# A fused attention and lookup block on one core: v projected in two portions around the first loads, its bias carried through the output projection

## The chip, the core and the metric

The kernel runs on one core of a Trainium2 chip. The metric is device time of one execution in microseconds (us); lower is better. Three runs of the kernel before gave 3075.67, 3077.20 and 3077.66 us, median 3077.2 us.

## The reference, cut to what matters

The input x is 4096 tokens of 256 channels. All arrays are float32.

```
xn  = layernorm(x)
q, k, v = split(xn @ w_qkv + b_qkv)          # 16 heads of 16 channels each
attn = softmax(q @ k.T / 4) @ v               # per head, 4096 x 4096 scores
y   = attn @ w_proj + b_proj
x   = x + layernorm(y)
h   = layernorm(x)                            # then a lookup in 1024 keys with the 8 best kept,
x   = x + layernorm(h + gate(h) * (softmax(top8(scores(h))) @ values))
```

The weights of a softmax row add up to 1, so a bias b_v added to every row of v comes out of the attention as b_v added to every row of attn. Hence (attn + b_v) @ w_proj + b_proj is attn @ w_proj + (b_v @ w_proj + b_proj).

## The kernel before, in words

The program of each engine is written out by hand, and the engines are tied by semaphores. Every engine works its program strictly in the order written. The token axis is cut into 32 tiles of 128 rows, and into 8 chunks of 4 tiles.

**First stage.** SP issues eight loads of x (L296), POOL issues the loads of w_qkv (L358), of the q and k bias (L359), and two broadcast loads of the v bias into `bv` (L361), then builds the identity and, from L388, the first 1/sqrt(variance) (`powers`, L380 and L382). DVE normalises a chunk (L748), TensorE transposes it (L1086), ACT keeps the transpose in `xnT` (L512), and TensorE projects q and k for it in four matrix products of two matmuls (`project_qk`, L1094). ACT evacuates each product twice (L520, L522), DVE takes the difference (L754), so that each of q and k is held as a rounded part and a rest, and SP stores both to DRAM (L302).

**Loads of the first head.** Scores and maxima are computed from stacks of such parts (`q_stack`, `k_stack`), read back from DRAM by `load_first` on SP: 12 transfers (L307), six of them for the maxima (semaphore `first_max_in`), then six for the scores (`first_score_in`).

**v.** Meanwhile ACT copies the normalised transposes into `v_src`, two buffers of one chunk (`copy_xnT`, L538), TensorE projects v (`project_v`, L1108: a loop over 8 chunks, with two pairs of tiles in each, four matmuls to a pair) into PSUM banks 4 and 5, and ACT evacuates each pair into `v_all` (`evacuate_v`, L544). POOL clears rows of the stacks (L398, L401), adds the bias to each pair of v tiles (L412), and copies the first head's v into `v_head` (`copy_v`, L405). All of v is projected before the first maximum.

**First maximum pass.** The softmax needs the maximum of each score row ahead of time. A piece is two matmuls of 512 columns (`max_half`, L1135) into one of two pairs of PSUM banks, and one reduction of 1024 columns on DVE (`row_max`, L797); 16 pieces and one small reduction (L804) make the 512 maxima of a query chunk. Before the main loop two whole chunks are done (AHEAD = 2), and half of the third (LEAD = 8 pieces): 40 pieces. POOL splits the negated maxima into three bf16 parts (`split_max`, L421 to L431) and TensorE puts them into rows (`max_row`, L1186), the first of them in bank 5, for which it waits on `v_evac`.

**Main loop.** 64 iterations (16 heads by 4 pairs of query chunks) of 32 steps. A step has two scores (L1161), two exponentials on ACT (L568), four products with v (L1170), and one further piece of a maximum (L1135, L797).

**Last iteration and second stage.** In the last iteration no maxima are left, and other work stands between the steps: `transpose_weights` (L1266 to L1269), `route_weights` (L1275, L1277), the transposes of attn, and `project_out` (L1294). DVE copies the weights out of PSUM (L948 to L954) and adds `bproj` to the projections (`projected`, L818). Then come the norms and the lookup to the end. The weights of this stage are loaded by SP behind `w3_init` (L327), which POOL raises as it fills small tensors (L449 to L454), more than 100 us ahead of their use.

Of the kernel before, what the change touches and what calls it, by code (L numbers as in the profile page):

```python
# [23 lines left out]
P = 128  # L24
# [10 lines left out]
def sandwich_kernel(nc, x, w_qkv, b_qkv, w_proj, b_proj, q_proj_w, router_w, aux_keys, aux_values,  # L35
# [46 lines left out]
        return S_BANK[(RING * it + at) % SRING]  # L82

    W3_LOADS = 14
    LOAD_EVERY = 4
    RUS = 64
    MASKROW = RD
# [6 lines left out]
    with ExitStack() as ctx:  # L94
# [3 lines left out]
        def sem(name):  # L98
            return ctx.enter_context(nc.semaphore(name))
# [29 lines left out]
        nm_parts = sb("nm_parts", [P, TPC, MROWS], BF16)  # L129
        rinv = sb("rinv", [P, 2, 4])  # L130
        lead = sb("lead", [P, 1])

        v_rows = v_all[:, :].rearrange("p (t c) -> p t c", c=C)

# [1 line left out]
        xn = work[:, 0:1024].rearrange("p (t c) -> p t c", t=TPC)  # L136
        wqkv = work[:, 2048:3584].rearrange("p (k n) -> p k n", k=CC)
        qk_f32 = k_raw[:, 0:4 * CH].rearrange("p (g t) -> p g t", g=4)
        bv = work[:, 3584:4096].rearrange("p (a c) -> p a c", a=2)
        bqk = work[:, 4096:4100]  # L140
        xnT = attn[:, 0:NC * CC * CH].rearrange("p (c k t) -> p c k t", c=NC, k=CC)
        v_src = [work[:, 1024 * b:1024 * (b + 1)].rearrange("p (k t) -> p k t", k=CC) for b in range(2)]
# [4 lines left out]
        hT = work[:, 5120:6144].rearrange("p (k t) -> p k t", k=CC)  # L147
        ru = work[:, 6144:6656]
        g1T = k_raw[:, 2048:2560]
        o2 = [work[:, 1024 * b:1024 * (b + 1)].rearrange("p (t c) -> p t c", t=TPC) for b in range(4)]  # L150
        res = [v.rearrange("p (t c) -> p t c", t=TPC) for v in (k_raw[:, 2560:3584], v_head_flat[:, 0:1024])]
        picked_flat = [q_raw[:, 1024 * (b + 2):1024 * (b + 3)] for b in range(2)]
# [57 lines left out]
        vsrc_ready = sem("vsrc_ready")  # L210
        v_ready = sem("v_ready")
        v_evac = sem("v_evac")
        v_biased = sem("v_biased")
        stack_in = [sem(f"stack_in{b}") for b in range(NB)]
        first_max_in = sem("first_max_in")
        first_score_in = sem("first_score_in")
# [76 lines left out]
        @block.sync  # L293
        def _(sp):
            for c in range(NC):
                sp.dma_start(x_sb[:, TPC * c:TPC * (c + 1), :], x_t[:, TPC * c:TPC * (c + 1), :]).then_inc(x_in[min(c, 2)], 16)  # L296

            with sp.Fori(0, NC) as c:
                for g in range(4):
                    sp.wait_ge(split_done, c * 4 + (g + 1 + CREDIT[split_done]))  # L300
                    dst = parts_dram[g // 2, :, (g % 2) * P:(g % 2 + 1) * P, bass.ds(c * CH, CH)]
                    sp.dma_start(dst.rearrange("r f t -> f r t"), qk_part[:, g, :, :]).then_inc(parts_out[g], 16)  # L302

            def load_first(slots, done):
                for n in slots:
                    for stack, qk, part in ((k_stack, 1, SLOT_K[n]), (q_stack, 0, SLOT_Q[n])):
                        sp.dma_start(stack[SLOT_ROW[n]:SLOT_ROW[n] + D, 1, 0:T].bitcast(F32),  # L307
                                     parts_dram[qk, part, 0:D, :]).then_inc(done, 16)

            def load_stack(h, b, after):  # L310
                for n, (row, pq, pk) in enumerate(zip(SLOT_ROW, SLOT_Q, SLOT_K)):
                    for m, (stack, qk, part) in enumerate(((k_stack, 1, pk), (q_stack, 0, pq))):
                        sp.wait_ge(pv_done, after + (2 * n + m) * LOAD_EVERY)
                        sp.dma_start(stack[row:row + D, b, 0:T].bitcast(F32), parts_dram[qk, part, h * D:(h + 1) * D, :]
                                     ).then_inc(stack_in[b], 16)

            for g in (0, 2, 1, 3):
                sp.wait_ge(parts_out[g], 16 * (NC + 1))
                if g == 2:
                    load_first((3, 4, 5), first_max_in)  # L320
                    load_first((0, 1, 2), first_score_in)
            load_stack(1, 0, 1 + CREDIT[pv_done])
            for h in range(2, H):
                load_stack(h, (h + 1) % NB, (h - 1) * PAIRS * KG + CREDIT[pv_done])

            sp.wait_ge(pv_done, (ITS - PAIRS) * KG + CREDIT[pv_done])
            sp.wait_ge(w3_init, 5)  # L327
            for dst, src in (
                (wproj, w_proj.rearrange("(k p) n -> p k n", p=P)),
                (bproj[:, 0, :], b_proj.partition_broadcast(P)),  # L330
                (bproj[:, 1, :], b_proj.partition_broadcast(P)),
                (keys, aux_keys.rearrange("(v p) d -> p v d", p=P)),
                (qpw, q_proj_w),
                (routw[0:RD, :], router_w),
                (u1w[0:F1, :], unc_w1),
                (rbias[RUS:RUS + F1, :], unc_b1.rearrange("(f a) -> f a", a=1)),
                (u2w[RUS:RUS + F1, :], unc_w2.rearrange("a f -> f a")),
                (u2b, unc_b2.partition_broadcast(P)),
                (gw, gate_w1.partition_broadcast(P)),
                (gb, gate_bias.partition_broadcast(P)),  # L340
                (rkT[MASKROW:MASKROW + 1, :], reliability_mask.rearrange("(a n) -> a n", a=1)),
                (values, aux_values.rearrange("(v p) d -> p v d", p=P)),
            ):
                sp.dma_start(dst, src, allow_slow_non_contiguous=True).then_inc(w3_in, 16)

            for p, (c, lo, hi) in enumerate(PIECES):
                if p < NC:
                    sp.wait_ge(res_ready, p + 1)
                else:
                    sp.wait_ge(last_ready, 1)  # L350
                sp.dma_start(out_t[:, TPC * c + lo:TPC * c + hi, :], res[c % 2][:, lo:hi, :]).then_inc(out_done[c % 2], 16)
            for b in range(2):
                sp.wait_ge(out_done[b], 16 * sum(c % 2 == b for c, _, _ in PIECES))
# [3 lines left out]
        def _(pool):  # L357
            pool.dma_start(wqkv, w_qkv.rearrange("(k p) n -> p k n", p=P)).then_inc(wqkv_in, 16)  # L358
            pool.dma_start(bqk, b_qkv[0:2 * C].rearrange("(g p) -> p g", p=P), allow_slow_non_contiguous=True).then_inc(w_in, 16)  # L359
            for a in range(2):  # L360
                pool.dma_start(bv[:, a, :], b_qkv[2 * C:3 * C].partition_broadcast(P)).then_inc(w_in, 16)  # L361
            pool.memset(minus_half[:], -0.5).then_inc(consts, 1)
            pool.memset(ident[:], 0.0).then_inc(consts, 1)
            pool.wait_ge(consts, 2)
# [40 lines left out]
                pool.tensor_copy(v_head[:, b, :, 0:D], v_rows[:, :, bass.ds(h * D, D)]).then_inc(vhead_ready, 1)  # L405


            with pool.Fori(0, NC) as c:
                for j in range(2):
                    pool.wait_ge(v_evac, c * 2 + (j + 1 + CREDIT[v_evac]))  # L410
                    pair = v_rows[:, bass.ds(c * TPC + 2 * j, 2), :]
                    pool.tensor_tensor(pair, pair, bv, ALU.add).then_inc(v_biased, 1)  # L412
            pool.wait_ge(v_biased, 2 * NC)
            copy_v(0, 1)

            def split_max(mi):
# [33 lines left out]
            pool.memset(ones, 1.0).then_inc(w3_init, 1)  # L450
            pool.memset(wcat, 0.0).then_inc(w3_init, 1)
            pool.memset(rbias, 0.0).then_inc(w3_init, 1)
            pool.wait_ge(w3_init, 4)
            pool.affine_select(out=rbias, in_=rbias, compare_op=ALU.not_equal, fill=float(RD) ** 0.5, base=-MASKROW,  # L454
                               pattern=[[-1, 1]], channel_multiplier=1).then_inc(w3_init, 1)
            with pool.Fori(H * NC - NC + AHEAD, H * NC) as c:
# [49 lines left out]
        def _(act):  # L506
# [16 lines left out]
                               bias=bqk[:, g:g + 1]).then_inc(f_ready, 1)  # L523

            move_xnT(0)
            act.wait_ge(w_in, 48)
            with act.Fori(0, NC - 1) as c:
                for g in range(4):
                    evacuate_qk(c, g)
# [195 lines left out]
        def _(dve):  # L725
# [217 lines left out]
            for it in range(ITS - 1):  # L943
# [9 lines left out]
            dve.tensor_copy(rkT[0:RD, :].rearrange("p (a n) -> p a n", a=2), ps[0:RD, 0:2, :]).then_inc(w3_e, 1)  # L953
            dve.tensor_copy(wcat[:, :, 0:RD], ps[:, 2, 2 * P:3 * P].rearrange("p (k n) -> p k n", k=CC)[:, :, 0:RD]  # L954
                            ).then_inc(w3_e, 1)
            combine_used(ITS - 1, PAIRS - 2, H - 1)
            projected(0, 0)
            projected(0, 1)
# [123 lines left out]
        def _(pe):  # L1082
# [15 lines left out]
            def xnT_block(c, k):  # L1098
                return xnT[:, bass.ds(c, 1), k, :].rearrange("p a t -> p (a t)")

            def project_v(c, b, j):

                pe.wait_ge(vsrc_ready, c + 1)
                pe.wait_ge(v_evac, c * 2 + (j + 1))
                for a in range(2):
                    i = 2 * j + a
                    for k in range(CC):
                        last = pe.matmul(ps[:, 4 + j, C * a:C * (a + 1)], v_src[b][:, k, P * i:P * (i + 1)],  # L1108
                                         wqkv[:, k, 2 * C:3 * C], start=(k == 0), stop=(k == CC - 1))
                last.then_inc(v_ready, 1)  # L1110

            pe.wait_ge(primed, 1)
            pe.wait_ge(xn_ready, TPC)
# [9 lines left out]
            for g in range(4):  # L1123
                project_qk(NC - 1, g)

            with pe.Fori(0, NC // 2) as c2:
                for b in range(2):
                    for j in range(2):
                        project_v(c2 * 2 + b, b, j)

            def max_half(k, e, mi, b1, c, slot):

# [110 lines left out]
            for c in range(AHEAD):  # L1243
                for k in range(16):
                    for e in range(2):
                        max_half(k, e, c, 1, c, k % 2)
            pe.wait_ge(v_evac, 2 * NC + CREDIT[v_evac])
            max_row(0, S_BANK[-2 % SRING])
            for k in range(LEAD):
# [11 lines left out]
            def transpose_weights():  # L1261

                pe.wait_ge(w3_in, 16 * W3_LOADS)
                pe.wait_ge(max_used, H * NC * 16 + CREDIT[max_used])
                for v in range(NV):
                    pe.transpose(ps[:, v // 4, P * (v % 4):P * (v % 4 + 1)], keys[:, v, :], ident[:, :])  # L1266
# [4 lines left out]
            def route_weights():  # L1271
# [4 lines left out]
                for k in range(CC):  # L1276
                    last = pe.matmul(ps[:, 2, 2 * P + HALF * k:2 * P + HALF * k + RD], qpw[:, P * k:P * (k + 1)], routT,  # L1277
                                     start=True, stop=True)
                last.then_inc(w3_t, 1)

            def attn_transpose(c, free, n):
# [59 lines left out]
            def aggregate(n):  # L1341
# [6 lines left out]
                for v in range(NV):  # L1348
# [7 lines left out]
                   {2: transpose_weights, 5: route_weights,  # L1356
                    7: lambda: attn_transpose(0, w3_e, 4),
                    9: lambda: project_out(0, 0, 2, w3_e, 5),
                    10: lambda: project_out(0, 1, 3, w3_e, 5),
                    11: lambda: attn_transpose(1, aT_ready, 1),  # L1360
                    13: lambda: project_out(1, 0, 2, y_evac, 1),
                    14: lambda: project_out(1, 1, 3, y_evac, 2),
# [88 lines left out]
```

## Time and profile before

| | |
|---|---|
| median of 3 runs | 3077.2 us (3075.67 to 3077.66) |
| the profiled execution's own time | 3076.01 us |
| its span | 3073.9 us |
| busy: PE, DVE, ACT, POOL | 98%, 91%, 82%, 8% |
| mean granted TensorE clock | 0.987 |
| first loads, norms, q and k | 0 to 82 us |
| v | 82 to 110 us |
| first maximum pass | 110 to 160.65 us |
| main loop with its last iteration | 160.65 to about 2795 us |
| the rest | about 2795 to 3073.9 us |

The times inside the span are counted from its start; 2.1 us of the execution's own time lie outside the span. The 2.4 GHz clock is written 1.00, the 1.2 GHz clock 0.50, and a stretch in which it changed has a value between. A busy TensorE is not a TensorE at its peak: at half clock it is busy for longer with the same work.

### The profile page before, as it was taken

The numbers are of one execution on the slowest core, as the hardware profiler recorded it, in microseconds if no ns is written. First come the engines' busy times: TensorE is split into PE (matmuls) and PEld (weight loads), VectorE is DVE, ScalarE is ACT, GpSimd is POOL, SyncE is SP. The second block draws the span as 40 slices with busy tenths as digits, with TensorE's granted clock in tenths as the row PEclk, the third lists the DMA queues.
The fourth block names the chain that finished last, engine by engine and source line by source line (L and its number), as shares of the span: only waits on it lengthen the run. The fifth ranks groups of instructions, "written<-read, shape, count | busy, mean of one in ns | idle before, by whom it ended". The sixth has DMA issues, their size and how long they took to land.

```text
span 3073.9 us, 67679 instructions
## 1 busy us (share of the span) xinstructions
PE 3023.7 (98%) x26807; PEld 1305.0 (42%) x26807; DVE 2802.0 (91%) x3050; ACT 2507.6 (82%) x4604; POOL 242.5 (8%) x793
## 2 busy tenths in 40 slices
PE   8999999999999999999999999999999999999997
PEld 4533333333333333333333333333333333345765
DVE  5599999999999999999999999999999999957776
ACT  6278888888888888888888888888888888874444
POOL 2400000000000000000000000000000000001012
PEclk9789999999999999999999999999999999999999
DMA  7420101010110101010202010101011010000001
GB/s 257 71 42 1 39 5 36 8 29 15 22 22 15 29 12 32 5 39 2 42 1 43 1 39 5 32 12 28 16 22 22 15 29 18 16 1 1 1 8 48
DMA packets 27399, 83.00 MB, mean 27 GB/s; under 512 B 4657, under 2 KB 15649, under 8 KB 24034
## 3 DMA queue, kind: packets, MB, share of 16 engines
q1 hardware_dynamic: 26834, 77.84, 10.9%
q8 instruction: 209, 3.42, 0.5%
q0 software_dynamic: 272, 1.05, 0.1%
q14 instruction: 84, 0.69, 0.1%
HBM read 57.90 MB, written 20.97 MB: 26 GB/s over the span
## 4 chain that ended last, share of the span: by engine, by line
PE 91%; DVE 4%; ACT 2%; issue 1%; POOL 0%; ACTq 0%; POOLq 0%; DVEq 0%
PE ps L1161 44%; PE ps L1170 37%; PE ps L1135 2%; PE ps L1094 2%; PE ps L1108 1%; PE ps L1186 1%; PE ps L1349 1%; PE ps L1086 1%; DVE partial L797 1%; PE ps L1294 1%; PE ps L1179 1%; DVE k_raw L868 1%; DVE q_raw L861 1%; ACT k_raw L642 1%; DVE q_raw L858 1%
## 5 line engine op out<-in xcount | busy, mean ns | idle before, releaser
L797 DVE TENSOR_REDUCE partial<-ps 128x1 f32<-128x1024 f32 x2048 | 2465.1, 1222 | 117.3 <-PE ps L1135 104.7
L568 ACT ACTIVATE work<-ps 128x512 f32<-128x512 f32 x4096 | 2206.9, 597 | 312.2 <-PE ps L1161 111.5
L1135 PE MATMUL ps<-k_stack,q_stack 48*128 48x512 f32 x4096 | 1533.0, 453 | 4.7 <-DVE partial L797 4.0
L1161 PE MATMUL ps<-q_stack,k_stack 64*128 64x512 f32 x4096 | 1507.8, 448 | 0.5 <-ACT work L568 0.5
L1170 PE MATMUL ps<-work,v_head 128*32 128x256 f32 x16384 | 1296.2, 391 | 0.0
L1161 PEld LDWEIGHTS ps<-q_stack,k_stack 64*128 64x128 f32 x4096 | 628.9, 184 | 812.1 <-ACT work L568 644.4
L1135 PEld LDWEIGHTS ps<-k_stack,q_stack 48*128 48x128 f32 x4096 | 635.7, 187 | 41.2 <-DVE partial L797 40.6
L1170 PEld LDWEIGHTS ps<-work,v_head 128*32 128x32 f32 x16384 | 329.1, 108 | 696.0 <-ACT work L568 595.2
L421 POOL CAST nm_parts<-negmax 128x4 bf16<-128x4 f32 x128 | 24.7, 193 | 2244.5 <-DVE negmax L804 2244.5
L1349 PE MATMUL ps<-k_raw,q_raw 128*128 128x256 f32 x512 | 122.3, 394 | 8.3 <-DVE attn L878 8.3
L560 ACT ACTIVATE q_stack<-ps 3x512 fp32r<-3x512 f32 x128 | 75.1, 587 | 52.5 <-PE ps L1186 49.5
L1349 PEld LDWEIGHTS ps<-k_raw,q_raw 128*128 128x128 f32 x512 | 98.4, 196 | 36.3 <-issue 17.7
L642 ACT ACTIVATE k_raw<-ps,q_raw 128x1024 f32<-128x1024 f32 x32 | 35.6, 1112 | 89.2 <-DVE q_raw L861 89.1
L868 DVE SCALAR_TENSOR_TENSOR k_raw<-q_raw,k_raw 128x1024 f32<-128x1024 f32 x32 | 39.4, 1232 | 29.1 <-ACT k_raw L642 29.1
L1328 PE MATMUL ps<-k_raw,work 64*128 64x512 f32 x128 | 65.2, 630 | 0.0
L1094 PE MATMUL ps<-attn,work 128*128 (+1 forms) x128 | 59.2, 617 | 1.3 <-ACT attn L512 1.3
L1186 PE MATMUL ps<-ident_bf,nm_parts 128*3 128x128 bf16 x512 | 49.9, 220 | 0.0
L1186 PEld LDWEIGHTS ps<-ident_bf,nm_parts 128*3 128x3 bf16 x512 | 36.1, 86 | 28.6 <-issue 1.3
L754 DVE TENSOR_TENSOR qk_part<-k_raw,qk_part 128x512 fp32r<-128x512 f32 x32 | 22.0, 691 | 25.2 <-ACT qk_part L522 25.2
L858 DVE MAX8 q_raw<-ps 128x8 f32<-128x1024 f32 x32 | 39.1, 1223 | 3.0 <-PE ps L1328 2.8
L861 DVE MATCH_REPLACE8 q_raw<-q_raw,ps 128x1024 f32<-128x1024 f32 x32 | 38.9, 1215 | 0.0
L650 ACT ACTIVATE q_raw<-ps 128x1024 f32<-128x1024 f32 x32 | 32.5, 1015 | 7.3 <-PE ps L1337 7.3
(126 smaller groups left out, 981.9 us busy)
## 6 DMA issues: line engine op xcount, KB each, us to landing
k_stack<-qk_parts SPq DMA_DIRECT2D x96, 256.0 KB, 4.2
q_stack<-qk_parts SPq DMA_DIRECT2D x96, 256.0 KB, 4.1
qk_parts<-qk_part SPq DMA_DIRECT2D x32, 512.0 KB, 2.8
x_sb<-L_attn_x SPq DMA_DIRECT2D x8, 512.0 KB, 10.3
out<-k_raw SPq DMA_DIRECT2D x4, 512.0 KB, 3.0
out<-v_head SPq DMA_DIRECT2D x3, 512.0 KB, 2.9
k_raw<-L_ffn_aux_values SPq DMA_DIRECT2D x1, 1024.0 KB
work<-L_attn_w_qkv POOLq DMA_DIRECT2D x1, 768.0 KB, 7.9
```

Of the source, the lines that this page charges most:

```text
L560: act.activation(q_stack[MROW:MROW + MROWS, b, bass.ds(c * CH, CH)], ps[0:MROWS, bank, :], ACT.Copy).then_inc(mrow_done, 1)
L568: act.activation(probs[:, g % DEPTH, a, :], ps[:, bank, :], ACT.Exp, scale=SCALE).then_inc(exp_done, 1)
L797: dve.tensor_reduce(partial[:, k // 4, k % 4:k % 4 + 1], ps[:, 2 * slot:2 * slot + 2, :], AX.XY, ALU.max).then_inc(max_used, 1)
L858: dve.max(top8[:, i, :], sc).then_inc(top_ready, 1)
L861: dve.match_replace(picked[n % 2], top8[:, i, :], sc, TAKEN).then_inc(picked_ready, 1)
L868: dve.scalar_tensor_tensor(out=wts_flat[n % 2], in0=picked_flat[n % 2], scalar=TAKEN, in1=wts_flat[n % 2], op0=ALU.is_equal, op1=ALU.mult, ...
L1094: last = pe.matmul(ps[:, 2 + g, :], wqkv[:, k, P * g:P * (g + 1)], xnT_block(c, k), start=(k == 0), stop=(k == CC - 1))
L1135: last = pe.matmul(ps[:, 2 * slot + e, :], q_stack[HALF:HALF + ROWS, b1, c * CH + (k // 4) * P:c * CH + (k // 4 + 1) * P], k_stack[HALF:HA ...
L1161: pe.matmul(ps[:, bank, :], k_stack[0:HALF, b, P * g:P * (g + 1)], q_stack[0:HALF, b, at:at + CH], start=True, stop=True).then_inc(s_ready, 1)
L1170: last = pe.matmul(ps[32 * i:32 * i + 32, O_BANK, 0:QH], v_head[:, b, g, :], probs[:, g % DEPTH, i // 2, QH * (i % 2):QH * (i % 2 + 1)], s ...
L1186: last = pe.matmul(ps[0:MROWS, bank, P * i:P * (i + 1)], nm_parts[:, i, :], ident_bf[:, :], start=True, stop=True)
L1349: last = pe.matmul(ps[:, 2, 0:C], wT[n % 2][:, v, :], values[:, v, :], start=(v == 0), stop=(v == NV - 1))
```

## The change

The v bias is no longer added to v. It is loaded as two columns (`bv`, 128 x 2) by one strided transfer where two broadcast ones stood; POOL spreads it to 128 x 256 (`bv_rows`) when it fills the small tensors of the second stage; two more matmuls in `route_weights` multiply it with w_proj, and DVE adds the product to `bproj`, behind which `project_out(0, 1)` waits. POOL's 16 additions over v are gone, and its copy of the first head's v waits for all evacuations instead.

`project_v` now does one tile (two matmuls). Tiles 0 to 11 are projected ahead of the first maximum pass; tiles 12 to 31 are written one behind each of the first 20 pieces of that pass (16 of the first chunk, 4 of the second). ACT's program for v is unchanged.

```
+    V_AHEAD = 12
+        bv = sb("bv", [P, CC])
-        bv = work[:, 3584:4096].rearrange("p (a c) -> p a c", a=2)
+        bv_rows = work[:, 4352:4352 + CC * P].rearrange("p (k m) -> p k m", k=CC)
...
SP:
-            sp.wait_ge(w3_init, 5)
+            sp.wait_ge(w3_init, 6)
...
POOL:
-            for a in range(2):
-                pool.dma_start(bv[:, a, :], b_qkv[2 * C:3 * C].partition_broadcast(P)).then_inc(w_in, 16)
+            pool.dma_start(bv[:, :], b_qkv[2 * C:3 * C].rearrange("(k p) -> p k", p=P), allow_slow_non_contiguous=True
+                           ).then_inc(w_in, 16)
...
-            with pool.Fori(0, NC) as c:
-                for j in range(2):
-                    pool.wait_ge(v_evac, c * 2 + (j + 1 + CREDIT[v_evac]))
-                    pair = v_rows[:, bass.ds(c * TPC + 2 * j, 2), :]
-                    pool.tensor_tensor(pair, pair, bv, ALU.add).then_inc(v_biased, 1)
-            pool.wait_ge(v_biased, 2 * NC)
+            pool.wait_ge(v_evac, 2 * NC + CREDIT[v_evac])
             copy_v(0, 1)
...
+            pool.tensor_copy(bv_rows, bv[:, :].unsqueeze(2).to_broadcast([P, CC, P])).then_inc(w3_init, 1)
+            pool.wait_ge(w3_init, 5)
...
ACT:
-            act.wait_ge(w_in, 48)
+            act.wait_ge(w_in, 32)
...
DVE:
+            dve.tensor_tensor(bproj, ps[:, 3, 0:C].unsqueeze(1).to_broadcast([P, 2, C]), bproj, ALU.add).then_inc(w3_e, 1)
+            dve.wait_ge(w3_e, 6)
             combine_used(ITS - 1, PAIRS - 2, H - 1)
...
PE:
+            def project_v(n):
+
+                c, j, a = n // TPC, n % TPC // 2, n % 2
+                b = c % 2
+                if a == 0:
+                    pe.wait_ge(vsrc_ready, c + 1)
+                    pe.wait_ge(v_evac, c * 2 + (j + 1))
+                for k in range(CC):
+                    last = pe.matmul(ps[:, 4 + j, C * a:C * (a + 1)], v_src[b][:, k, P * (n % TPC):P * (n % TPC + 1)],
+                                     wqkv[:, k, 2 * C:3 * C], start=(k == 0), stop=(k == CC - 1))
+                if a == 1:
+                    last.then_inc(v_ready, 1)
...
-            with pe.Fori(0, NC // 2) as c2:
-                for b in range(2):
-                    for j in range(2):
-                        project_v(c2 * 2 + b, b, j)
+            for n in range(V_AHEAD):
+                project_v(n)
...
                 for k in range(16):
                     for e in range(2):
                         max_half(k, e, c, 1, c, k % 2)
+                    if V_AHEAD + 16 * c + k < NT:
+                        project_v(V_AHEAD + 16 * c + k)
...
+                pe.wait_ge(w3_init, 6)
...
+                for k in range(CC):
+                    last = pe.matmul(ps[:, 3, 0:C], bv_rows[:, k, :], wproj[:, k, :], start=(k == 0), stop=(k == CC - 1))
                 last.then_inc(w3_t, 1)
...
-                    10: lambda: project_out(0, 1, 3, w3_e, 5),
+                    10: lambda: project_out(0, 1, 3, w3_e, 6),
```

## Rows read from the trace of the kernel before

**Rows 1.** The page: span, busy time of each engine, the chain's shares by engine.
```profile
span 3073.9 us, 67679 instructions
...
PE 3023.7 (98%) x26807; PEld 1305.0 (42%) x26807; DVE 2802.0 (91%) x3050; ACT 2507.6 (82%) x4604; POOL 242.5 (8%) x793
...
PE 91%; DVE 4%; ACT 2%; issue 1%; POOL 0%; ACTq 0%; POOLq 0%; DVEq 0%
```
**Rows 2.** Busy time by stretch: stretch, length, PE, PEld, DVE, ACT, POOL, clock, DMA, GB/s.
```profile
300.00:2700.00 2400.00, 2399.79 (x23290) 947.68 (x23288) 2315.92 (x2129) 2132.35 (x4019) 125.60 (x609) 1.00 0.10 21
```
**Rows 3.** The chain, 0 to 260 us: start, length, engine, tensor, line, instructions.
```profile
13.36 6.51 PE ps L1094 x8
...
20.74 6.87 PE ps L1094 x16
...
81.10 0.95 ACT work L538
82.18 27.89 PE ps L1108 x128
...
115.50 1.23 PE ps L1135 x2
...
160.72 0.72 PE ps L1161
```
**Rows 4.** DMA issues of SP in order of time: the first and sixth load.
```profile
83.10 0.36 SPq L307 DMA_DIRECT2D k_stack<-qk_parts  x1
...
85.36 0.42 SPq L307 DMA_DIRECT2D q_stack<-qk_parts  x1
```
**Rows 5.** Time to landing (last column, us) of those two issues.
```profile
k_stack<-qk_parts SPq DMA_DIRECT2D x1, 256.0 KB, 5.2
...
q_stack<-qk_parts SPq DMA_DIRECT2D x1, 256.0 KB, 14.6
```
**Rows 6.** Busy time by stretch, columns as in rows 2: where the clock changes.
```profile
79.80:82.20 2.40, 0.02 (x1) 0.03 (x1) 1.00 (x2) 2.37 (x4) 0.26 (x1) 1.00 0.87 329
...
110.07:114.80 4.73, 3.00 (x10) 1.47 (x10) 3.97 (x4) 0.60 (x1) 4.73 (x5) 0.98 0.04 5
114.80:160.65 45.85, 42.87 (x82) 18.02 (x80) 43.08 (x39) 0.59 (x1) 4.16 (x13) 0.50 0.00 0
160.65:169.25 8.60, 8.60 (x41) 3.74 (x44) 5.81 (x6) 5.71 (x11) 0.00 (x0) 0.50 0.15 32
...
2795.20:2797.80 2.60, 0.24 (x2) 0.27 (x2) 2.26 (x7) 2.55 (x4) 0.00 (x0) 0.94 0.00 0
2797.80:2807.90 10.10, 10.10 (x27) 6.67 (x28) 4.95 (x11) 2.94 (x3) 0.00 (x0) 0.51 0.00 0
```
**Rows 7.** TensorE in order of time: start, length, line, instructions, idle before.
```profile
110.00 1.18 PE L1135 MATMUL ps<-k_stack,q_stack 48*128 48x512 f32 x4
112.11 0.73 PE L1135 MATMUL ps<-k_stack,q_stack 48*128 48x512 f32 x2 [0.93 <-DVE partial L797]
...
2804.94 3.36 PE L1294 MATMUL ps<-k_raw,aT 128*128 128x256 f32 x8
```
**Rows 8.** Groups by line, 110.1 to 160.6 us.
```profile
L797 DVE TENSOR_REDUCE partial<-ps 128x1 f32<-128x1024 f32 x40 | 47.5, 1221 | 31.7 <-PE ps L1135 31.1
```
**Rows 9.** POOL and DVE in order of time, 2 to 7.5 us.
```profile
2.25 0.78 POOL L359 DMA_DIRECT2D work<-L_attn_b_qkv  x1
3.03 1.09 POOL L361 DMA_DIRECT2D work<-L_attn_b_qkv  x2
...
7.11 0.23 POOL L380 TENSOR_SCALAR veps<-mv 128x4 f32<-128x4 f32 x1 [1.85 <-DVE mv L735]
...
6.27 0.38 DVE L735 BATCH_NORM_AGGREGATE mv<-stats 128x2 f32<-128x6 f32 x4
```
**Rows 10.** All engines in order of time, 2722 to 2753 us.
```profile
2738.96 1.99 PE L1294 MATMUL ps<-k_raw,aT 128*128 128x256 f32 x8
2740.99 0.69 DVE L818 TENSOR_TENSOR v_all<-ps,k_raw 128x512 f32<-128x512 f32 x1 [4.60 <-PE ps L1294]
```

More of the change, by code:

```diff
@@ L212, in sandwich_kernel @@
         v_evac = sem("v_evac")
-        v_biased = sem("v_biased")
         stack_in = [sem(f"stack_in{b}") for b in range(NB)]
@@ L452, in _ @@
             pool.memset(rbias, 0.0).then_inc(w3_init, 1)
-            pool.wait_ge(w3_init, 4)
+            pool.tensor_copy(bv_rows, bv[:, :].unsqueeze(2).to_broadcast([P, CC, P])).then_inc(w3_init, 1)
+            pool.wait_ge(w3_init, 5)
             pool.affine_select(out=rbias, in_=rbias, compare_op=ALU.not_equal, fill=float(RD) ** 0.5, base=-MASKROW,
@@ L1099, in xnT_block @@
                 return xnT[:, bass.ds(c, 1), k, :].rearrange("p a t -> p (a t)")
[L1101 to L1110, printed above, removed]
+            def project_v(n):
[9 more added lines that the diff above has]
+                    last.then_inc(v_ready, 1)
             pe.wait_ge(primed, 1)
```

## The prediction, as put on record before the change was run

> **What bounds the kernel now.** I read the page first, to see whether one engine sets the time: TensorE is busy for 98% of the span and makes up 91% of the chain that ended last [rows 1]. Then the busy time of the main loop: in 2400 us of it TensorE is busy for 2399.8 us, DVE for 2315.9 us, at full clock [rows 2]. The change touches no step of that loop but the last iteration, so its gain and its cost lie before 160.65 us and in some microseconds near 2732 us. So I went to the chain of the first 260 us. It runs through q and k, waits for ACT's copy of the transposes (0.95 us), then takes 27.89 us for v (128 records, two to each of 64 matmuls: 0.436 us for a matmul, 0.872 us for a tile), then goes to and fro between TensorE and DVE in the maximum pass until the first score at 160.7 us [rows 3]. v stands on the path with all its length. The last question is what TensorE would wait for if v were shorter. That is the sixth load, on which the maximum pass depends: issued at 85.36 us, landed 14.6 us later, at 99.96 us [rows 4, 5].
>
> In the maximum pass the reader should look at the clock. It fell 4.7 us after v had ended, in a stretch in which TensorE had work for 3.00 of 4.73 us, and stayed at 1.2 GHz for 45.85 us, until dense work had run from 160.65 to 169.25 us [rows 6]. This cost the pass almost nothing: a reduction on DVE takes 1.221 us, 40 of them nearly fill the 50.6 us from 110.07 to 160.65, and a pair of matmuls takes 1.23 us even at half clock [rows 3, 8]. DVE paces the pass, at 50.6 / 40 = 1.265 us a piece. TensorE's free time there is what the change wants to use. It is there only at full clock.
>
> **v ahead of the pass.** Twelve tiles take 12 x 0.872 = 10.5 us and end at 82.18 + 10.5 = 92.6 us; 20 x 0.872 = 17.4 us leave the front. The wait that is late next is the sixth load: TensorE idles from 92.6 to 100.0 us, 7.3 us. Queued behind that wait is its whole program, and DVE and ACT (but for the last evacuation) have nothing else. So the pass starts 10.1 us earlier, not 17.4. The loads are issued by SP behind its stores, which the change leaves alone.
>
> **One interleaved piece.** At full clock: four max matmuls took 1.18 us, the first of two with its fill 0.73 us [rows 7]. So a further matmul costs (1.18 - 0.73) / 2 = 0.23 us, a pair 0.46 us in a dense stream and at most 0.73 us. With a tile of v a piece takes 1.33 to 1.60 us; I take 1.40, near the lower end, since weights load beside running matmuls and nothing waits. It is above DVE's 1.22 us, so TensorE paces these 20 pieces. At half clock a pair takes about 1.18 us (the 1.23 us of [rows 3] less some fill), and v's kind of matmul (128 x 256, float32, four of them in 3.36 us [rows 7]) 0.84 us, so a tile 1.67 us: 2.85 us a piece.
>
> **The clock after the wait.** The trace holds one idle gap of this kind that is shorter: 2.4 us before 2797.6 us, after which the clock was low for 10.1 us under steady work; another of 2.4 us, at 80 us, did not lower it [rows 6]. An empty stretch of 7.3 us is three times either and longer than the 4.7 us of thin work before the fall at 114.8. I take it that the pass starts at 1.2 GHz. How long it stays there: 10.1 us and 8.6 us in two places of [rows 6]. At the start of the kernel eight records of L1094 took 6.51 us where later sixteen took 6.87 us [rows 3], so the clock was half for about 5.9 us of dense work there, though no granted clock is recorded for it. Mean 8.2 us; bounds 5.9 and 10.3 us. In 8.2 us 2.9 pieces are done; the other 17.1 take 23.9 us. The interleaved part ends at 100.0 + 8.2 + 23.9 = 132.1 us.
>
> The Trainium skill ("TensorE: Matmul & The Clock Gate", section "HAM oscillation — how this bites in real kernels") speaks against this change: a wait for a transfer between bursts of matmuls lets the clock fall to half, and the next burst starts cold. The fall at 2797.8 us agrees; the gap at 80 us shows that not every short wait does it. By the rule the wait costs its own length and the slow pieces after it, as summed here; without it, the 7.35 us of the first rival.
>
> **The rest of the pass.** 20 pieces at DVE's pace, 1.265 us: 25.3 us, to 157.4 us in place of 160.65: 3.25 us gained. The clock will again be low by the end, as before, so the first steps of the main loop cost what they did. ACT's evacuations and copies of v now have more time for each pair than before (two pieces). The bank of the first row of maxima waits for v's evacuation, done at about 133 us, and is used after the second chunk, at about 147 us. POOL's split of the first maxima now stands behind its wait for all of v and the copy of one head; it is done at about 135 us, and DVE asks for it at the end of the second chunk only. POOL's 16 additions went beside other work, and save nothing.
>
> **The start.** POOL issues one strided transfer for two broadcast ones: 1.09 us goes, and 0.54 to 0.78 us comes (half of L361, or the q and k bias [rows 9]). POOL computes the first power at 7.11 us, while the variance was there at 6.65 us, so at most 0.2 us can be gained; nothing is lost unless the transfer is slower than all of these. I take 0.1 us.
>
> **The second stage.** Two more matmuls of 128 x 256: by v's pace 0.87 us, by L1294 (1.99 us for four with its fill [rows 10]) up to 1.0 us. TensorE works without a pause there, so they lie on the path: 0.9 us lost. A slip can be absorbed by the 2.4 us gap at 2795 only if what it waits for does not slip, and that is ACT's work on the same chain; bounds 0.6 and 1.0 us. DVE's addition (as L818, 0.69 us) and its wait come before L818 at 2740.99 us, for which DVE had idled 4.6 us [rows 10]: covered; uncovered it would cost 0.7 us. POOL's fill of `bv_rows` and the loads behind it have some 100 us of slack.
>
> **Sum.** -3.25 - 0.1 + 0.9 = -2.45 us. The profiled execution has 3076.01 us (span 3073.9), so 3073.6 us; it stood 1.2 us under the median of the runs, 3077.2, and the median after is 3074.7 us.
>
> **Rivals.** First, the clock does not fall in the wait (for it: the gap at 80 us, with the clock held). The 20 pieces take 28.0 us, the first score comes at 153.3 us, 7.35 us earlier, and the net is -6.55 us: 3070.65 us. Against it: 7.3 us is three times that gap.
>
> Second, on the other side, the clock falls and does not come back while tiles of v are interleaved. For it: in the pass before, with TensorE busy for 42.87 of 45.85 us, it did not return [rows 6]. Against: there TensorE waited for DVE at every piece; here it has work without a gap, and under such work the clock did come back at 13 to 20 us and at 2798 to 2808 us. The price: 20 x 2.85 = 57.0 us, so the interleaved part ends at 157 us, the first score comes at 182.3 us, and the net is +22.4 us: 3099.6 us. A microsecond at half clock costs 1 - 1.40 / 2.85 = 0.51 us, so it decides from the point where the clock has been low for 13 us (net zero), and the time is measurably longer from 25 us.
>
> Third, a full-clock piece takes 1.60 us, since each change between the two kinds of matmul shows its fill: 3.4 us more, net +1.0 us, 3078.2 us. [rows 7] bound it from that side.
>
> Fourth, more comes out than summed: the sixth load lands earlier, or the low clock near 2800 us, which the shifted times could shorten, goes; 10.1 us at half clock held about 5 us. Net -7 to -8 us, about 3069.5 us. Nothing speaks for it but that those falls depend on gaps of about 2 us.
>
> **How the numbers follow.** Forecast as summed (cold for 5.9 to 10.3 us): 0.62; its own range is 3073.3 to 3076 us from the time at half clock and about 1 us more on each side from the pace of a piece and the run. First rival 0.12, second 0.05, third 0.13, fourth 0.08. A measurement of this kernel tells 0.2% from no change, 6.2 us: below 3071.0 us is faster, above 3083.4 us slower. Faster: nearly all of the first and the fourth, less what noise brings back: 0.18. Slower: the second and a little for what I have not seen: 0.06. The same: 0.76. The range that leaves out two in ten goes from 3069.0 us, into the fourth rival, to 3079.0 us, over the third.
>
> **What would show it.** In the profile after: v ends near 92.6 us in its first portion; TensorE idle until 100.0 us for L1135; granted clock 0.50 over 6 to 10 us behind it, then 1.00 to about 132 us; 20 pieces at 1.33 to 1.60 us, then 1.265 us; the first score (L1161) near 157.4 us; the q_raw copy behind `route_weights` 0.9 us later against the steps before it. The forecast is wrong if the clock is at 1.00 throughout from 100 to 130 us or at 0.50 beyond 113 us, if the first max matmul starts before 98 or after 102 us, or if the iterations between 300 and 2700 us change their length at all.

## The result: 28 us slower, and where they are in the profile after

| | before | after |
|---|---|---|
| median of six runs each | 3077.62 us | 3105.37 us (3103.26 to 3107.50) |
| ratio | | 1.0087, 95% interval 1.0074 to 1.0100 |
| profiled execution: its own time, span | 3076.01, 3073.9 us | 3105.48, 3103.7 us |
| mean granted TensorE clock | 0.987 | 0.978 |
| first score, from the chain or TensorE's rows | 160.65 us | 187.90 us |
| first transpose of `transpose_weights` | 2724.86 us | 2750.92 us |

The forecast was 2.5 us faster (3077.2 to 3074.7 us); the clock took the course of the second rival instead. The page of the kernel after (against [rows 1]): TensorE is still busy for 98% and makes up 91% of the chain, and DVE has as much work as before. The shares tell nothing. What does is easy to pass over: TensorE is busy for 26.4 us more with four records more, so the same work ran slower, and DMA, which had no share of the chain, has 1% of it.

```profile
span 3103.7 us, 67608 instructions
...
PE 3050.1 (98%) x26811; PEld 1316.9 (42%) x26811; DVE 2803.0 (90%) x3051; ACT 2508.9 (81%) x4604; POOL 224.1 (7%) x777
...
PE 91%; DVE 4%; ACT 2%; issue 1%; DMA 1%; POOL 0%; SPq 0%; ACTq 0%; DVEq 0%; POOLq 0%
```

The busy time by stretch of the kernel after (against [rows 2, 6]; third from the right is the granted clock) tells it:

```profile
79.20:81.30 2.10, 0.00 (x0) 0.00 (x0) 0.82 (x2) 2.10 (x4) 0.13 (x1) 1.00 0.84 318
81.30:86.40 5.10, 5.08 (x16) 4.19 (x17) 0.00 (x0) 1.51 (x2) 5.10 (x1) 0.67 1.14 240
86.40:93.60 7.20, 7.20 (x34) 6.03 (x32) 0.00 (x0) 4.28 (x6) 7.20 (x2) 1.00 0.96 109
93.60:98.88 5.28, 0.03 (x1) 0.00 (x0) 0.00 (x0) 1.54 (x2) 1.36 (x1) 0.72 1.17 130
98.88:161.95 63.07, 63.07 (x120) 33.46 (x121) 24.67 (x21) 8.21 (x12) 0.00 (x0) 0.50 0.17 19
161.95:187.90 25.95, 23.85 (x49) 10.72 (x48) 22.93 (x21) 1.18 (x2) 3.14 (x12) 0.50 0.00 0
187.90:194.90 7.00, 7.00 (x33) 3.05 (x32) 5.53 (x5) 5.03 (x9) 0.00 (x0) 0.50 0.00 0
300.00:2700.00 2400.00, 2399.80 (x23294) 947.84 (x23286) 2316.38 (x2129) 2133.88 (x4020) 128.02 (x615) 1.00 0.10 21
```

TensorE had nothing to do from 93.6 to 98.88 us, and the clock fell in that gap. Then came 63.07 us in which TensorE was busy without a pause at half clock. There are two low clocks here with opposite ends: the one from about 82.4 to 85.8 us, under v alone (a mean of 0.67 in the second row), was over in 3.4 us; the other lasted through everything to 194.9 us. The main loop is the same.

TensorE in order of time, the kernel after (start, length, line, instructions, idle before):

```profile
81.32 12.31 PE L1108 MATMUL ps<-work 128*128 128x256 f32 x48 [2.30 <-ACT work L535]
98.88 1.22 PE L1134 MATMUL ps<-k_stack,q_stack 48*128 48x512 f32 x2 [5.25 <-DMA q_stack<-qk_parts]
100.03 2.07 PE L1108 MATMUL ps<-work 128*128 128x256 f32 x4
102.04 1.22 PE L1134 MATMUL ps<-k_stack,q_stack 48*128 48x512 f32 x2
...
161.95 2.07 PE L1134 MATMUL ps<-k_stack,q_stack 48*128 48x512 f32 x4
164.49 2.35 PE L1134 MATMUL ps<-k_stack,q_stack 48*128 48x512 f32 x4 [0.46 <-DVE partial L794]
```

A piece with a tile takes 102.04 - 98.88 = 3.16 us, 20 of them 63.07 us; then come 20 plain pieces at 1.30 us. The sum by place: the first score is 27.25 us later; 1.19 us come back in the main loop, up to 0.8 of them (an estimate: half of 1.6 us) at its start, where the clock returned 7.0 us behind the first score instead of 8.6; the last iteration is 0.93 us longer; and the second stage of this execution is 2.8 us longer. Together that is 29.8 us of span. In that stage the low clock near 2830 us lasted 13.7 us where it was 10.2, and with the shorter ones behind it TensorE worked at half clock for some 25 us against 20.4 before.

### The profile page after: what moved, and what is told of

It is laid out like the page before. It is cut to its first block, busy times and chain, and to the rows that moved or that the text cites. A ratio compares the mean times of both kernels' runs of the same rounds, so it can differ in the third digit from the quotient of the medians.

```text
span 3103.7 us, 67608 instructions
## 1 busy us (share of the span) xinstructions
PE 3050.1 (98%) x26811; PEld 1316.9 (42%) x26811; DVE 2803.0 (90%) x3051; ACT 2508.9 (81%) x4604; POOL 224.1 (7%) x777
## 3 DMA queue, kind: packets, MB, share of 16 engines
q1 hardware_dynamic: 26834, 77.84, 10.8%
## 4 chain that ended last, share of the span: by engine, by line
PE 91%; DVE 4%; ACT 2%; issue 1%; DMA 1%; POOL 0%; SPq 0%; ACTq 0%; DVEq 0%; POOLq 0%
PE ps L1160 43%; PE ps L1169 37%; PE ps L1134 3%; PE ps L1093 2%; PE ps L1108 1%; PE ps L1353 1%; PE ps L1185 1%; PE ps L1085 1%; PE ps L1298 1%; PE ps L1178 1%; DVE k_raw L865 1%; DVE q_raw L858 1%; ACT k_raw L639 1%; DVE q_raw L855 1%; PE ps L1313 1%
## 5 line engine op out<-in xcount | busy, mean ns | idle before, releaser
L541 ACT ACTIVATE v_all<-ps 128x512 f32 (+1 forms) x16 | 9.6, 597 | 65.2 <-PE ps L1108 65.2
L1108 PE MATMUL ps<-work 128*128 128x256 f32 x128 | 53.8, 580 | 2.3 <-ACT work L535 2.3
L1108 PEld LDWEIGHTS ps<-work 128*128 128x128 f32 x128 | 33.7, 283 | 21.4 <-issue 13.0
```

## The experiments

Two theories stood against each other once the trace was read. In the first, the gap lowers the clock, and the stream of pieces with tiles can hold full clock but not win it back. In the second, the stream itself lets the clock fall, with or without a gap. All times of first scores below are from the profiled executions; ratios are to the kernel before on the same chip. The bias stays moved in all of them.

### The bias alone

```
-    V_AHEAD = 12
+    V_AHEAD = 32
```

> The changed kernel, but with all 32 tiles of v ahead of the first maximum pass, as before the change: what is left is the move of the bias. Both theories on the clock expect the same: first score at about 160.5 us, the last iteration 0.9 us longer, so about 3078.5 us (0 to 2 us above the kernel before). If moving the bias costs anything else, the time is above 3082 us.

Measured: 3078.10 us, ratio 1.0004 (0.9995 to 1.0013), first score at 160.89 us. The bias is not the cause. In the kernel after, the two added matmuls and DVE's addition stand like this (against [rows 10]):

```profile
2758.09 0.65 PE L1279 MATMUL ps<-q_raw 128*128 128x48 f32 x4
2758.58 1.10 PE L1282 MATMUL ps<-k_raw,work 128*128 128x256 f32 x4
...
2761.02 0.67 DVE L953 TENSOR_TENSOR k_raw<-ps,k_raw 128x512 f32<-128x512 f32 x1
...
2767.99 0.69 DVE L815 TENSOR_TENSOR v_all<-ps,k_raw 128x512 f32<-128x512 f32 x1 [4.53 <-PE ps L1298]
```

DVE still idles 4.53 us ahead of `projected`, so its addition is covered, as forecast.

### No gap: 20 tiles ahead

```
-    V_AHEAD = 12
+    V_AHEAD = 20
```

> The changed kernel with 20 tiles of v ahead of the pass instead of 12, so that v ends at about 98.8 us, just as the sixth load lands (98.9 us after the change), and 12 tiles interleaved. Theory 1 (the clock falls in the wait, and an alternating stream holds full clock but can't win it back): granted clock 1.00 through the interleaved pieces, 1.33 to 1.60 us each, first score at about 151 us, 3069 us. Theory 2 (the alternating stream itself lets the clock fall, gap or no gap): the clock falls some 5 us into the pass, pieces of 3.15 us from there, first score at about 166 us, 3084 us.

Measured: 3074.48 us, ratio 0.9989 (0.9980 to 0.9998), first score at 156.98 us. The clock was full through all 12 pieces with tiles, as theory 1 has it. The gain is 5 us smaller than expected: a piece takes 102.40 - 100.68 = 1.72 us, not 1.40, which is 3.8 us for 12, and v ended at 100.68 us since the clock had dipped behind the 2.3 us gap ahead of v. TensorE in this kernel:

```profile
100.68 0.73 PE L1134 MATMUL ps<-k_stack,q_stack 48*128 48x512 f32 x2
101.34 1.13 PE L1108 MATMUL ps<-work 128*128 128x256 f32 x4
102.40 0.73 PE L1134 MATMUL ps<-k_stack,q_stack 48*128 48x512 f32 x2
```

### The gap filled, everything else as in the change

```
             for n in range(V_AHEAD):
                 project_v(n)
+            for n in range(7):
+                for k in range(CC):
+                    pe.matmul(ps[:, O_BANK, 0:C], ident[:, :], wqkv[:, k, 2 * C:3 * C], start=(k == 0), stop=(k == CC - 1))
```

> The changed kernel (12 tiles ahead, 20 interleaved) with the wait of 5.3 us for the sixth load filled by 14 matmuls of 128 x 256 whose product in PSUM nobody reads. Theory 1: the clock stays at 1.00 through all 20 pieces, first score at about 152 us, 3070 us. Theory 2: it falls some 5 us into the pass and stays low, first score at about 181 us, 3098 us.

Measured: 3077.22 us, ratio 0.9999 (0.9989 to 1.0008), first score at 159.28 us. 14 matmuls that compute nothing take 28 us off the kernel. Order and number of the pieces and tiles are those of the change; busy time of the 20 pieces with tiles:

```profile
99.67:134.10 34.43, 34.43 (x120) 19.43 (x120) 24.39 (x21) 8.21 (x12) 0.00 (x0) 1.00 0.31 34
```

34.43 us at 1.00 in place of 63.07 at 0.50. Theory 2 has fallen. The 7 us to the expectation are again the piece: 20 x (1.72 - 1.40) = 6.4 us.

### The gap left, the other 20 tiles in one go behind it

```
             pe.wait_ge(first_max_in, 16 * LOADS // 2)
+            for n in range(V_AHEAD, V_AHEAD + 20):
+                project_v(n)
+            v_behind = {}
```

> 12 tiles ahead, the same wait of 5.3 us for the sixth load, and then the other 20 tiles of v in one go ahead of the first piece. Theory 1 (dense v wins the clock back, the alternating stream doesn't): half clock for 3 to 10 us behind the wait, then full; v ends at about 119 us, first score at about 169 us, 3087 us. Theory 3 (after so long a gap nothing wins it back for tens of us): v ends at 132 us or later, first score at 183 us, 3101 us.

Measured: 3085.04 us, ratio 1.0026 (1.0016 to 1.0036), first score at 168.08 us. v alone wins the clock back in 3.4 us after a gap of 5.26 us:

```profile
98.27:101.70 3.43, 3.40 (x8) 2.77 (x9) 0.00 (x0) 0.00 (x0) 0.00 (x0) 0.50 0.96 110
101.70:117.42 15.72, 15.72 (x73) 13.55 (x73) 0.00 (x0) 8.21 (x12) 0.00 (x0) 1.00 0.48 52
```

### Blocks of four instead of one by one

```
+            v_behind = {3: 4, 7: 4, 11: 4, 15: 4, 19: 4}
```

`v_behind` gives the number of tiles of v behind a piece.

> The changed kernel (12 tiles ahead, the same wait), with the other 20 tiles in five blocks of four, each behind four pieces, instead of one behind each piece: the same matmuls, a quarter of the changes between the two kinds. Theory 1a (v alone, some 3 us or more in one go, wins the clock back, as it did in 3.3 us in the run with 20 tiles in one go; alternation with the maxima prevents it): clock back within the first or second block of v, then held; interleaved part some 40 us instead of 63, first score at about 163 us, 3080 us. Theory 1b (once the maxima have begun at half clock, nothing short of a long stretch without them wins it back): half clock throughout, first score at 185 us or later, 3103 us.

Measured: 3089.88 us, ratio 1.0031 (1.0019 to 1.0043), first score at 169.85 us. Neither side is quite right: the clock came back in the first block of v, near 109.2 us, fell again among the next four pieces (112.7 us), returned in the second block (119.5 us), held through the third and fourth, fell at 140.2 us and came back in the last block (143.5 us). Blocks give a chance to win it back and one to lose it: four pieces in a row leave TensorE waiting for DVE (0.85 and 0.40 us in the rows below). Behind pieces run at half clock v needed longer than the 3.4 us it needs behind an idle gap: 5.8 us in the first block and 5.1 us in the second. Start of the first three blocks of pieces and tiles:

```profile
98.56 2.07 PE L1134 MATMUL ps<-k_stack,q_stack 48*128 48x512 f32 x4 [5.11 <-DMA q_stack<-qk_parts]
101.16 2.35 PE L1134 MATMUL ps<-k_stack,q_stack 48*128 48x512 f32 x4 [0.53 <-DVE partial L794]
103.44 6.62 PE L1108 MATMUL ps<-work 128*128 128x256 f32 x16
109.99 1.19 PE L1134 MATMUL ps<-k_stack,q_stack 48*128 48x512 f32 x4
112.03 0.73 PE L1134 MATMUL ps<-k_stack,q_stack 48*128 48x512 f32 x2 [0.85 <-DVE partial L794]
113.16 1.22 PE L1134 MATMUL ps<-k_stack,q_stack 48*128 48x512 f32 x2 [0.40 <-DVE partial L794]
114.31 6.31 PE L1108 MATMUL ps<-work 128*128 128x256 f32 x16
...
124.37 3.72 PE L1108 MATMUL ps<-work 128*128 128x256 f32 x16
```

### What in the stream fails to win the clock back

First the maxima's own matmuls, in one go behind the gap:

```
             pe.wait_ge(first_max_in, 16 * LOADS // 2)
+            for n in range(40):
+                pe.matmul(ps[:, O_BANK, :], q_stack[HALF:HALF + ROWS, 1, 0:P], k_stack[HALF:HALF + ROWS, 1, 0:CH],
+                          start=True, stop=True)
```

> The changed kernel with 40 extra matmuls of the maxima's own kind (48 of 128 rows, 512 columns, result not read) in one go behind the wait, ahead of the first piece. If it is the changes between the two kinds (weights that load in the open) that keep the clock low, this dense stream wins it back in 3 to 10 us and the 20 interleaved pieces of 1.72 us hold it: first score at about 171 us, 3089 us. If it is the maxima's matmuls themselves, with 48 rows, that don't win it back, the clock stays at 0.50 through them (0.59 us each, 23.6 us) and behind them: first score at about 211 us, 3129 us.

Measured in one run: 3124.98 us, first score at 204.58 us. Busy time by stretch of this kernel (the 40 matmuls, then the 20 pieces with tiles):

```profile
98.50:115.74 17.24, 17.24 (x41) 13.25 (x42) 0.00 (x0) 0.00 (x0) 0.00 (x0) 0.50 0.61 67
115.74:178.80 63.06, 63.06 (x122) 33.45 (x121) 24.66 (x21) 8.26 (x13) 0.00 (x0) 0.50 0.00 0
```

17.24 us of matmuls without a gap (0.43 us each, 0.59 expected) did not bring the clock back, where v had needed 3.4 us. So changes between kinds are not needed to explain it. Whether they have a part in it besides is not shown. What remained was the form: rounded data with one record to a matmul where v's has two, or 48 rows. This pair tells them apart, with v's kind of matmul and only the rows varied:

```
+            for n in range(20):
+                pe.matmul(ps[:, O_BANK, 0:C], ident[64:112, :], wqkv[64:112, 0, 2 * C:3 * C], start=True, stop=True)
...
+                pe.matmul(ps[:, O_BANK, 0:C], ident[0:128, :], wqkv[0:128, 0, 2 * C:3 * C], start=True, stop=True)
```

> The changed kernel with 20 extra matmuls of v's kind (float32, 256 columns, result not read) behind the wait and ahead of the first piece, but over 48 of the 128 rows. If the number of rows at work decides whether the clock comes back, it stays at 0.50 through them (0.84 us each, 16.8 us) and behind them: first score at about 204 us, 3122 us. If it is the data type or the single pass of the maxima's matmuls that fails to win it back, the clock returns in 3 to 7 us as under v, and the interleaved pieces hold it: first score at about 169 us, 3086 us.

> The same 20 extra matmuls over all 128 rows. Expected by every theory but the one that nothing wins the clock back: 1.00 after 3 to 7 us, held through the 20 interleaved pieces of 1.72 us, first score at about 169 us, 3086 us.

Measured, one run each: 3126.85 us with 48 rows, 3089.68 us with 128; first scores at 205.06 and 170.16 us. Busy time with 48 rows:

```profile
99.00:115.90 16.90, 16.90 (x41) 13.27 (x41) 0.00 (x0) 0.00 (x0) 0.00 (x0) 0.50 0.68 75
115.90:178.90 63.00, 63.00 (x122) 33.55 (x120) 24.66 (x21) 8.20 (x12) 0.00 (x0) 0.50 0.00 0
```

and with 128 rows:

```profile
99.49:103.80 4.31, 4.31 (x11) 3.48 (x12) 0.00 (x0) 0.00 (x0) 0.00 (x0) 0.54 1.01 114
103.80:110.30 6.50, 6.50 (x32) 5.46 (x30) 0.00 (x0) 0.00 (x0) 0.00 (x0) 1.00 0.91 98
110.30:144.60 34.30, 34.30 (x121) 19.45 (x120) 24.28 (x21) 8.20 (x12) 0.00 (x0) 1.00 0.01 1
```

The same instruction, type, column count and density: with 48 rows half clock for 16.90 us and behind it, with 128 rows full clock after 4 us and held through the 20 pieces. For a stream of one kind, then, the rows at work decide whether the clock comes back, as far as one run of each can tell. The maxima and the run with 48 rows both use rows 64 to 111, so how many rows and which rows are not told apart. This run is also the change with a cure that leaves the gap where it is; it pays 10.8 us for it.

### Two versions that are faster

The sparse one puts one tile behind every second piece, where DVE leaves room:

```
-    V_AHEAD = 12
+    V_AHEAD = 20
...
+            v_behind = {0: 1, 2: 1, 4: 1, 6: 1, 8: 1, 10: 1, 12: 1, 14: 1, 16: 1, 18: 1, 20: 1, 22: 1}
```

> 20 tiles of v ahead of the pass, and the other 12 behind every second piece (0, 2, ..., 22) instead of behind each of the first 12. At full clock a piece with a tile takes 1.72 us and one without 0.5 to 0.7, 2.3 us for two, under DVE's 2.45: DVE would pace them and v would be free. If the clock holds through this stream (TensorE busy for some nine tenths of it), first score at about 151 us, 3068 us. If it falls as in the pure maximum pass, two pieces take some 4.4 us at half clock: first score at about 170 us, 3088 us.

Measured: 3069.09 us, ratio 0.9970 (0.9958 to 0.9982), first score at 150.51 us. The clock held to 131 us and fell among the plain pieces:

```profile
100.19:131.00 30.81, 29.03 (x98) 15.55 (x98) 28.15 (x26) 6.05 (x9) 0.95 (x3) 1.00 0.34 38
131.00:150.50 19.50, 17.94 (x38) 7.73 (x38) 18.38 (x17) 0.59 (x1) 2.17 (x9) 0.53 0.00 0
```

The last is the sparse one with added matmuls over all rows whose product nobody reads, in a bank that holds no data then. They stand ahead of v, while ACT copies, behind each of pieces 24 to 39, and in the second stage:

```
+            def keep_busy(n, w):
+                for _ in range(n):
+                    pe.matmul(ps[:, O_BANK, 0:C], ident[:, :], w, start=True, stop=True)
...
+            keep_busy(5, wqkv[:, 0, 2 * C:3 * C])
...
+                        keep_busy(1, wqkv[:, 0, 2 * C:3 * C])
...
+                keep_busy(1, wqkv[:, 0, 2 * C:3 * C])
...
             combine(ITS, S_BANK[2])
+            keep_busy(5, wproj[:, 0, :])
             learn(0, 2, y_evac, 7)
```

> As the sparse form, and with matmuls of 128 x 256 whose product nobody reads where TensorE would idle or work thinly: five in the 2.3 us ahead of v, one behind each of the last 16 pieces of the pass, five in the 2.4 us wait of the second stage. If it is only idle and thin stretches that lower the clock, it stays at 1.00 from 20 us to the second stage and through it: first score at 150 us, the first steps of the main loop 2 us shorter, 5 us less in the second stage, about 3061 us. If the sparse stream itself lets the clock fall, this comes out near the sparse form or above it, 3085 us or more.

Measured: 3063.04 us, ratio 0.9948 (0.9935 to 0.9962), first score at 149.50 us. Busy time of the whole pass, of the start of the second stage, of the low clock behind it, and of the rest of the span:

```profile
100.00:149.50 49.50, 48.31 (x165) 24.25 (x163) 46.78 (x42) 5.20 (x9) 3.15 (x12) 1.00 0.20 22
...
2788.00:2802.00 14.00, 12.70 (x60) 8.31 (x59) 11.29 (x23) 6.70 (x7) 0.00 (x0) 0.99 0.00 1
2801.70:2805.10 3.40, 3.40 (x8) 1.63 (x7) 3.22 (x12) 0.48 (x1) 1.27 (x2) 0.51 0.00 0
2788.48:3065.20 276.72, 249.18 (x1126) 180.68 (x1126) 206.21 (x499) 122.52 (x143) 41.73 (x59) 0.95 0.05 16
```

The clock is full through the pass and through the work that had it low for 10.1 us in [rows 6] (here 2788 to 2798 us). It still fell at 153 us, in the first steps of the main loop, among three short idle times of TensorE (0.73 us together, for ACT's copy into `q_stack` and for reductions), and came back near 160 us, so those 2 us were not gained. Nor were the 5 us of the second stage: the clock fell later in it instead, first from 2801.7 to 2805.1 us, and from the end of the filled wait at 2788.48 us to the end of the span this execution took 276.7 us, the kernel before 276.3 us from the same point. The profiled execution, at 3066.99 us the slowest of the five, is 9.0 us under that of the kernel before; the first score, 11.15 us earlier, makes up more than all of it. What the other 5 us of the median come from is not shown.

## Why the prediction was wrong, step by step

**The steps ahead of the pass** held in kind: the wait is there, with 5.25 us of idle time (7.3 forecast), since the load landed at 98.9 us and v's first part ended at 93.6, late by the clock's dip behind the 2.3 us gap. That gap had not lowered the clock in the kernel before [rows 6].

**The clock falls in the wait**: right.

**"How long it stays there: ... mean 8.2 us; bounds 5.9 and 10.3 us"** is the step that failed. The clock stayed at half through all 63.07 us of the interleaved part, and beyond it. I took three recoveries from the trace as a property of TensorE being without a gap and carried them over to this stream. (The first of them is also a little long: its two rows give 2 x 6.51 - 6.87 = 6.15 us, where 5.9 was written. It changes nothing.)

The pair with 48 and 128 rows shows that being without a gap is not enough: half clock for all 16.90 us with 48 rows, against about 4 us with 128. None of the three recoveries was under matmuls over 48 rows alone. At the start of the kernel they are projections over 128 rows. Behind the first score a score over 64 rows and a maximum over 48 run at the same time, as their equal start times show, with products over 128 rows between them. In the second stage there are products over 64 and 128 rows:

```profile
160.65 0.79 PE L1161 MATMUL ps<-q_stack,k_stack 64*128 64x512 f32 x1
160.65 0.79 PE L1135 MATMUL ps<-k_stack,q_stack 48*128 48x512 f32 x1
...
2797.56 1.84 PE L1317 MATMUL ps<-q_raw,k_raw 64*128 64x1 f32 x8 [2.40 <-ACT k_raw L635]
2799.33 1.97 PE L1337 MATMUL ps<-ident,k_raw 128*128 128x128 f32 x8
2801.23 3.78 PE L1328 MATMUL ps<-k_raw,work 64*128 64x512 f32 x4
```

The trace of before held the warning in one row [rows 6]: TensorE busy for 42.87 of 45.85 us, nearly all of it with 48-row matmuls, and half clock throughout. I explained that row away by its small gaps, and gave this course 5 in 100; the run with 40 maxima in one go shows half clock without those gaps.

Why the changed stream as a whole does not win the clock back stays open. It has 48-row matmuls in 1.15 of each 3.15 us and v over 128 rows in the rest. The average of rows does not explain it: weighted by time it is about 99 here, and about 95 in the 10.1 us of the second stage, under which the clock came back (estimates from the times of the records). The order may matter: the 10.1 us of the second stage end with 3 us over 128 rows in a row, and the clock came back inside blocks of v in the run with blocks of four, while the changed stream has 2.0 us of v at a time. Against that, behind the first score the products over 128 rows come in no longer stretches (1.9 us), but between pairs that use 112 rows at once. No run varies this by itself.

**The price of that rival** was 22.4 us; the result is 27.75. The piece at half clock more than makes up the difference: 3.15 us where 2.85 were summed (20 x 0.30 = 6.0 us). Four records of v take 2.00 us there against 1.67 for four of the same kind in a row. I had taken both kinds at the pace they have among themselves. The same error is in the full-clock piece, 1.72 us against 1.40, above the bound of 1.60: 0.66 us to the next kind and 1.06 us for v's four records, where v alone needs 0.87. At both clocks the excess over the summed streams is 0.3 to 0.4 us a piece: that is what alternating the two kinds costs by itself.

**The rest of the pass and its length** held: 25.95 us for 20 plain pieces (25.3). **The bias**: 0.93 us in the last iteration (0.9), DVE's addition covered, and 3078.10 us by itself, within what a measurement tells from no change. **The main loop** between 300 and 2700 us: unchanged.

Even with the clock saved, the change as it stands is worth nothing (3077.22 us): the 17.4 us taken from the front go into 20 x (1.72 - 1.265) = 9.1 us of slower pieces, the 7 us from the end of v's first part to the sixth load, and the bias. That it is close to the price of the third rival (3078.2 us) is luck: that sum had 8.2 us of half clock and pieces of 1.60 us, this run has none there and pieces of 1.72.

## What to carry to other kernels

Before an engine is made to wait for a load that its work used to cover, look at what runs behind the wait. Here the same 5 us gap was followed by 3.4 us of half clock where matmuls over all rows came next, and it cost 28 us of run time where the stream behind it took a third of its time for matmuls over 48 of 128 rows. Take the clock's return only from rows with the same kind of work, and look for stretches where it did not return although the engine was busy.

If matmuls over part of the rows must follow a wait, fill the wait (this took the 28 us off), or place full-array work between the wait and them (20 such matmuls took 10.8 us and saved 16); and put extra work only behind as many steps as the pacing engine leaves room for.

## What the runs showed of the chip that I had not expected

- Full and half clock are not symmetric: the same 20 pieces ran at 1.00 for 34.43 us when they were entered at full clock, and at 0.50 for 63.07 us when they were entered at half.
- Full-density matmuls over 48 rows did not raise the clock in 16.90 us (float32) or 17.24 us (the maxima's kind); over 128 rows it rose within about 4 us (and in 3.43 us under v). Behind maxima run at half clock v needed 5.8 and 5.1 us.
- The gap of 2.3 us ahead of v lowered the clock in the profiled executions of eight kernels (the kernel after and the bias alone among them) and not in three (the kernel before, the filled gap, the sparse one), with the same instructions on both sides of it. Each time v won it back in about 3.4 us; its first 12 tiles took 12.31 us in place of 10.63, so it cost 1.7 us. What decides between the two courses is not shown.
- A change of kind in a dense stream costs: 1.72 us for a pair and a tile that take 0.46 and 0.87 us among their own kind.
